# One pass with a running maximum for two 16-head cross attentions

## The reference

```python
# L0: 8 heads of 64, keys turned by their place, keys and values projected from the normed context
sim = einsum('bhid,bhjd->bhij', q, k);  attn = softmax(sim);  out = einsum('bhij,bhjd->bhid', attn, v)
# L1: 16 heads of 16
kp, vp = ctx @ wk.T + bk, ctx @ wv.T + bv
scores = einsum('bhqd,bhkd->bhqk', qh, kh) / 4 - 10000.0 * (1.0 - mask[:, None, None, :])
# L2: 8 heads of 128, no softmax: a cosine of f_q and f_k mixed with products of variances
# L3: 16 heads of 16, no projections: keys and values are the context itself
sim = einsum('bhqd,bhkd->bhqk', q, k) / 4 + (-1e9) * (~mask)[:, None]
```

## Time and profile before

| what | us |
|---|---|
| median of three runs (lowest, highest) | 3203.61 (3202.01, 3211.06) |
| the profiled run, its time | 3209.38 |
| its span, first to last instruction | 3207.2 |
| TensorE busy | 2561.2 (80%) |
| VectorE busy | 1870.5 (58%) |
| ScalarE busy | 1337.1 (42%) |
| GpSimd busy | 563.4 (18%) |
| mean granted TensorE clock | 0.914 of 2.4 GHz |

### The profile page before, as it was taken

The page is one execution under the profiler, slowest core; times in us unless marked ns, Lnnn a source line. Parts: engine busy times, 40 slices in busy tenths (PEclk is TensorE's granted clock), DMA queues, the critical chain, the costliest instruction groups (busy, mean ns, idle before and its releaser), DMA issues. The chain is left out here.

```text
span 3207.2 us, 58901 instructions
## 1 busy us (share of the span) xinstructions
PE 2561.2 (80%) x22154; PEld 1560.7 (49%) x22154; DVE 1870.5 (58%) x2677; ACT 1337.1 (42%) x1802; POOL 563.4 (18%) x331
## 2 busy tenths in 40 slices
PE   3488789999747676799984789999953588699987
PEld 3333346666446232366653645655643333356546
DVE  7599877777662798611114178878847699611111
ACT  2277642222232566467761222222201365466652
POOL 0044420000001343200000023343312244100000
PEclk7799999999879999899995999999976799899999
DMA  7455634443125335467742410100010345568746
GB/s 232 140 182 182 217 104 103 103 94 88 51 69 184 120 119 149 115 138 160 160 97 73 168 47 23 34 23 23 12 39 28 117 141 154 136 148 174 164 103 212
DMA packets 251728, 370.92 MB, mean 116 GB/s; under 512 B 30116, under 2 KB 222055, under 8 KB 251517
## 3 DMA queue, kind: packets, MB, share of 16 engines
q1 hardware_dynamic: 251648, 369.83, 41.5%
HBM read 292.07 MB, written 77.71 MB: 115 GB/s over the span
## 5 line engine op out<-in xcount | busy, mean ns | idle before, releaser
L1870 PE MATMUL l2x_kf<-l2x_w,l2x_nin 128*128 128x512 f32 x784 | 340.5, 594 | 4.2 <-DVE l2x_f L1821 3.4
L1915 POOL TENSOR_TENSOR l2x_gk<-l2x_f,l2x_ks 128x1024 f32<-128x1024 f32 x98 | 182.3, 1896 | 830.2 <-DVEq L1846 830.2
L1180 ACT ACTIVATE l1x_att_pt<-l1x_att_ps,l1x_mask_col 128x1024 f32<-128x1024 f32 x196 | 218.1, 1113 | 99.7 <-PE l1x_att_ps L1235 95.4
L1183 ACT ACTIVATE l3x_att_pt<-l3x_att_ps 128x1024 f32<-128x1024 f32 x196 | 200.4, 1023 | 103.2 <-PE l3x_att_ps L1239 103.0
L1856 ACT ACTIVATE l2x_fsq<-l2x_f 128x1024 f32<-128x1024 f32 x98 | 103.6, 1057 | 330.0 <-DVE l2x_f L1821 330.0
L1870 PEld LDWEIGHTS l2x_kf<-l2x_w,l2x_nin 128*128 128x128 f32 x784 | 147.7, 190 | 188.5 <-issue 180.9
L1172 ACT ACTIVATE l0x_att_pt<-l0x_att_pt 128x1024 f32<-128x1024 f32 x99 | 104.7, 1057 | 300.4 <-DVE l0x_att_pt L1119 300.4
L658 DVE TENSOR_REDUCE l1x_max_red<-l1x_max_ps 128x2 f32<-128x896 f32 x196 | 203.8, 1079 | 37.9 <-PE l1x_max_ps L836 36.7
L815 PE MATMUL l0x_max_pk<-l0x_max_xin,l0x_wk 128*128 128x448 f32 x448 | 197.4, 566 | 29.8 <-DMA l0x_max_xin<-scratch_nT 14.8
L836 PE MATMUL l3x_max_ps<-l3x_max_kp,l3x_qb 128*128 128x448 bf16 x448 | 162.9, 364 | 64.6 <-DVE l3x_max_red L658 26.3
L1140 DVE TENSOR_TENSOR l1x_att_v<-l1x_att_pv,l1x_bv 128x256 f32<-128x256 f32 x98 | 41.6, 424 | 291.6 <-PE l1x_O L1260 281.0
(11 more groups left out here) (689 smaller groups left out, 5259.9 us busy)
## 6 DMA issues: line engine op xcount, KB each, us to landing
l1x_att_kt<-scratch_KS SPq DMA_DIRECT2D x84, 448.0 KB, 8.9
l3x_att_kt<-scratch_KS SPq DMA_DIRECT2D x84, 448.0 KB, 8.6
scratch_KT<-l0x_max_kf SPq DMA_DIRECT2D x28, 896.0 KB, 5.5
l0x_att_kt<-scratch_KT SPq DMA_DIRECT2D x56, 448.0 KB, 7.1
scratch_KS<-l1x_max_kp SPq DMA_DIRECT2D x28, 672.0 KB, 3.7
scratch_KS<-l3x_max_kp SPq DMA_DIRECT2D x28, 672.0 KB, 3.5
l0f_w<-L_ffn_exp_w SPq DMA_DIRECT2D x16, 1024.0 KB, 6.1
l1f_w<-L_ffn_W SPq DMA_DIRECT2D x16, 1024.0 KB, 6.4
```

The costliest lines, as they stand in the source:

```text
L1180: ins = act.activation(pt[u][:, :, :], psc[u][:, :, :].rearrange("p a (b q) -> p (a b) q", q=P), ACT.Exp, bias=tile_ap)
L1183: ins = act.activation(pt[u][:, :, :], psc[u][:, :, :].rearrange("p a (b q) -> p (a b) q", q=P), ACT.Exp)
L1870: last = pe.matmul(pf[u][:, n, :], nin[b][:, c, t * P:(t + 1) * P], w[:, c, n * BANK:(n + 1) * BANK], start=(c == 0), stop=(c == DC - 1))
L1915: pool.tensor_tensor(gk[b][:, t, :, 0:HD], f[b][:, t, :].rearrange("p (h d) -> p h d", h=H), ks[b][:, 2, t, :].unsqueeze(2).broadcast_to([ ...
```

## The change

- `find_maximum` and `attend` are no longer called for L1 and L3. A new class `Heads16` makes one pass of 14 chunks with a running maximum. A chunk has 28 slots of four heads (exponentials of 512 elements). In between stand 16 maximum units a chunk, spread over slots 0, 1, 3, 5, 7, 8, 10, 12 of each half: eight for the later half of the next chunk's heads, eight for the first half of the chunk after it. A unit is one head against 896 keys: two matmuls of 32 rows, in two row groups and two banks, and one fused add (of the mask) and maximum on VectorE, which starts from the maximum so far.
- Once a chunk the new maximum is turned, split and sent through DRAM into the second of two query stacks; the exponential of the difference is spread by four matmuls, copied out by ScalarE, and VectorE multiplies `O` by it before the first weighing of the chunk.
- The bf16 scores for the maxima come from the high part of the keys, loaded from DRAM. So the parts of L1's keys are made ahead, in the loop of the 8-head attention's `attend` (class `SplitKeys`, with its projection), and those of L3 in the loop of the third cross attention. There each has one set of buffers.
- The rows of ones are filled by GpSimd in the setup blocks. The query rows go to two buffers. The mask parts of L1 and `mask3` fall away; the mask's bias goes to DRAM and comes back per chunk, spread over all partitions. In L3 the values are copied by GpSimd, a chunk at a time.

```diff
 class QueryRows:
...
-        parts_to_rows(sp, self.rows, self.scratch, PARTS_OF_Q, self.S.sem("q_in"))
+        for rows in self.rows:
+            parts_to_rows(sp, rows, self.scratch, PARTS_OF_Q, self.S.sem("q_in"))
...
 def attend(...)          # sync: the loads of the next chunks
+                side.load(sp, 0)
                 with sp.Fori(0, steps - 1) as i:
                     for b in range(2):
+                        side.spill(sp, 2 * i + b)
+                        side.load(sp, 2 * i + b + 1)
                         after(sp, sem(f"chunk_used{b}"), i + 1)
...
+                side.finish(sp, 2 * steps)
                          # scalar, behind the exponential of tile t
+                        m, s = 2 * i + t // TILES, t % TILES
+                        if 2 <= s < 6:
+                            side.evacuate(act, m, s - 2)
+                        if s in (3, 5):
+                            side.high(act, m, (s - 3) // 2)
+                        if s == 6:
+                            side.middle(act, m)
                          # tensor
                         weigh(i, t, o)
+                        if 1 <= t % TILES < 5:
+                            side.project(pe, 2 * i + t // TILES, t % TILES - 1)
                          # gpsimd
+                with pool.Fori(0, steps) as i:
+                    for b in range(2):
+                        side.subtract(pool, 2 * i + b)
...
+SLOTS = 4 * TILES
+SPLIT = CHUNK // 2
+HALF_UNITS = 8
+UNIT_SLOTS = tuple(n * SLOTS // 2 // HALF_UNITS for n in range(HALF_UNITS))
+GAP_SLOT, TURN_SLOT, FACTOR_SLOT = SLOTS // 2, 15, 19
+class SplitKeys:
...
+    def load(self, sp, m):
+        if self.proj:
+            after(sp, self.sem("projected"), 4 * m)
+        else:
+            after(sp, self.sem("rest"), m)
...
+        sp.dma_start(self.xin[:, :, :], self.src[bass.ds(m, 1)].squeeze(0)).then_inc(self.sem("xin"), 16)
+    def spill(self, sp, m):
+        after(sp, self.sem("low"), m + 1)
...
+        sp.dma_start(self.dst[bass.ds(m, 1)].squeeze(0), self.kp[:, :, :, :].rearrange(
+            "p s c k -> p (s c) k")).then_inc(self.sem("spilled"), 16)
+    def project(self, pe, m, n):
+        c, side = n // 2, n % 2
+        if n == 0:
+            after(pe, self.sem("xin"), (m + 1) * 16)
+        after(pe, self.sem("read"), 4 * m + n)
+        for d in range(DC):
+            last = pe.matmul(self.px[:, 0:SPLIT], self.w[:, d, c * P:(c + 1) * P],
+                             self.xin[:, d, side * SPLIT:(side + 1) * SPLIT], start=(d == 0), stop=(d == DC - 1))
...
+    def high(self, act, m, c):
+        if c == 0:
+            after(act, self.sem("spilled"), m * 16)
...
+        act.activation(self.kp[:, 0, c, :], self.kf[:, c, :], ACT.Copy).then_inc(self.sem("high"), 1)
+    def middle(self, act, m):
+        after(act, self.sem("rest"), m + 1)
+        act.activation(self.kp[:, 1], self.rest[:, :, :], ACT.Copy).then_inc(self.sem("middle"), 1)
+    def subtract(self, pool, m):
+        after(pool, self.sem("high"), (m + 1) * DC)
+        after(pool, self.sem("low"), m)
+        pool.tensor_tensor(self.rest[:, :, :], self.kf[:, :, :], self.kp[:, 0], ALU.subtract).then_inc(
+            self.sem("rest"), 1)
+        after(pool, self.sem("middle"), m + 1)
+        pool.tensor_tensor(self.kp[:, 2], self.rest[:, :, :], self.kp[:, 1], ALU.subtract).then_inc(
+            self.sem("low"), 1)
...
+class Heads16:
...
+    def ones_rows(self, pool):
+        for b in range(2):
+            pool.memset(self.kt[b][STACK:STACK + 3, :, :], 1.0)
...
+                    def top_to_rows(i, b):          # sync
...
+                        sp.dma_start(rows_dram.rearrange("n h q -> h n q"), parts[:, :, :]).then_inc(
+                            sem("rows_out"), 16)
+                        after(sp, sem("rows_out"), (m + 1) * 16)
+                        sp.dma_start(q_rows[b][STACK:STACK + 3].rearrange("n h q -> n (h q)"),
+                                     rows_dram.rearrange("n h q -> n (h q)")).then_inc(sem(f"rows{b}"), 16)
...
+                    def maximum(i, b, x):           # vector
...
+                        after(dve, sem(f"maxima{x % 2}"), units // 2 * m + x // 2 + 1)
...
+                        dve.tensor_tensor_reduce(junk[x % 2][:, :, :], pm[x % 2][:, :, 0:SPLIT],
+                                                 mrow[b][:, :].rearrange("p (s k) -> p s k", s=2), 1.0,
+                                                 top[1 - b][:, x:x + 1], ALU.add, ALU.max,
+                                                 top[b][:, x:x + 1]).then_inc(sem("max_read"), 1)
...
+                    def body(i, b):
...
+                        after(dve, sem("weighed1"), per * m)
+                        after(dve, sem("F"), m)
+                        dve.tensor_tensor(O[:, :], O[:, :], F[:, :], ALU.mult).then_inc(sem("rescaled"), 1)
...
+                    def body(i, b):                 # scalar
+                        m = 2 * i + b
+                        for s in range(SLOTS):
+                            weights(i, b, s)
+                            if s == TURN_SLOT and exists(i, b, 1):
+                                after(act, sem("gap"), m + 1)
+                                act.activation(fac[:, :, :], gap[:, :].unsqueeze(2).broadcast_to([P, H, 32]),
+                                               ACT.Exp).then_inc(sem("fac"), 1)
+                            if s == FACTOR_SLOT and exists(i, b, 1):
...
+                                act.activation(F[:, :], px[:, :], ACT.Copy).then_inc(sem("F"), 1)
...
+                    def max_unit(i, b, x):          # tensor
...
+                        c, g = x // 8, x % 8 // 2
+                        for side, stationary in enumerate((qb, qb_turned)):
+                            at = (32 * g + 64 * side) % P
+                            last = pe.matmul(pm[x % 2][:, side, 0:SPLIT], stationary[c][at:at + 32, x % 8, :],
+                                             high[b][at:at + 32, c, side * SPLIT:(side + 1) * SPLIT], start=True,
+                                             stop=True)
...
+                    def body(i, b):
...
+                        for s in range(SLOTS):
+                            if s + 1 < SLOTS:
+                                scores(i, b, s + 1)
...
+                            if s in UNIT_SLOTS and exists(i, b, 1):
+                                max_unit(i1, b1, HALF_UNITS + UNIT_SLOTS.index(s))
+                            if s - SLOTS // 2 in UNIT_SLOTS and exists(i, b, 2):
+                                max_unit(*ahead(i, b, 2), UNIT_SLOTS.index(s - SLOTS // 2))
...
+                            weigh(i, b, s)
...
 def l2_xattn(...)        # sync, behind the load of nin for the chunk
+                            side.load(sp, 2 * i + b)
+                            side.spill(sp, 2 * i + b)
```

529 lines of the change are left out of this document (432 added, 97 removed).

## The result

The change makes the kernel a little slower: 3220.7 us (median of 8 runs, 3209.8 to 3226.0) beside 3205.4 us for the kernel before on the same chip, a ratio of 1.0041 with a 95% interval of 1.0027 to 1.0054. The forecast was 3169 us, 35 us faster. The profiled run has a span of 3218.8 us, 11.6 over that of before.

The account below looks back on a forecast made before the run. 16-head maximum passes were taken as VectorE-bound, weighing and 8-head attention as TensorE-bound. Second -118 and set-up +16, fourth -94 and set-up +26, 8-head +130, third +5: -35 us from 3203.6, so 3169 us, own range 3115 to 3225.

Parts of the forecast that it names:

- the wait for `xin`: 8-head attention: next load queues behind the spill, so TensorE stands 2.5 us in 13 chunks, 33 us, bounds 0 and 65.
- what the loop turn gives: 8-head attention: unsized allowance taken off the wait, 38.4 us of chain against a chunk of 35.6, leaving 2.5.
- The projections: 8-head attention: four key projections added to each chunk on TensorE, 6.6 us a chunk, 92 us in all.
- The ends of the stage: 8-head attention: tail of the last spill, 5 us.
- Loop turns and chunk starts: Second attention: TensorE's loss at loop turns and chunk starts, 1.0 us of each 34.5 us chunk.
- Slots, units, the fused reduction, the order of bounds: 16-head loops: slots 0.66 and 0.88 us, maximum unit 0.30, fused add and maximum 1.15; VectorE's work hidden behind TensorE.
- The set-up's 26 us: Fourth attention's set-up: VectorE's chain waits for both GpSimd memsets of the ones rows, 26 us more.
- Third, +5: Third attention: no TensorE work added, but the second chunk's load comes late at the start, +5 us.
- VectorE's sums beside GpSimd's subtractions: 8-head attention: VectorE's sums stand while GpSimd subtracts, with about 3.5 us slack per tile; put at nothing.
- Rival 1: 16-head loops: a maximum unit's two halves run one after the other, 85 less 5 us, 3249 us; chance 0.13.
- Rival 2: 16-head attentions: the fused reduction runs at half speed, 2.0 us, deciding from about 1.8; 3282 us; chance 0.06.
- Rival 3: 8-head attention: the load of `xin` arrives in time, -33 us, 3136 us; chance 0.17.

Follow-up runs that it names:

- only the fourth's half: Kernel before plus one pass in the fourth attention and its key parts in the third's loop, 8-head and second unchanged: 3137.7 us, ratio 0.9780.
- load first: Kernel after, with SyncE issuing the next chunk's key load before it waits for the low part and stores: 3145.2 us, ratio 0.9805.

## Why the prediction was wrong

**The direction** is wrong, by two terms of the sum, both about what stops TensorE between its operations, neither about an operation. They took 62 us, and the fourth attention, 17 us better than forecast, hid a part of it; by that luck the time still lies in the forecast's own range of 3115 to 3225.

- **8-head, the wait for `xin`: mis-sized.** The step "TensorE stands 2.5 us in each of 13 chunks, 33 us, bounds 0 and 65" measured 5.0 us a chunk, 65 us. The chain itself was right: from the fourth projection to the store's issue 13.2 us where the forecast's parts make 13.0, store and load to the next projection 8.7 where they make 8.4. Most of what it left out is the clock: behind the gap the next tile runs 1.6 us slower, and that tile is part of the chain. The two small differences of the chain make 0.5 of the missing 2.5 us, and another 0.3 is what the forecast took off for "what the loop turn gives", which no row shows. The projections, 6.6 us a chunk, measured 6.5. The ends of the stage were 5 in the sum and are about 13.
- **Second, "Loop turns and chunk starts", of which "I keep 1.0 of it a chunk": wrong in kind.** It was taken over from a loop of 1523 instructions that had no fetch at its turns between 1400 and 1635. The new body of 1721 is fetched again at each turn, 3.4 to 4.5 us in which TensorE stands and the slow clock behind it. ScalarE's table load stands at the turns of both kernels, but only in the new one do the turns take longer for it (TensorE waits 1.3 us where no fetch covers it). Mean distance of chunks 36.2 us for 34.5. With TensorE's and ScalarE's loops written out it is 33.0, so the turns cost 3.2 us a chunk where 1.0 stood in the sum. All terms of operations together were 0.5 us too high, and the forecast had the stage right but for this.
- **Slots, units, the fused reduction, the order of bounds:** right, to 0.02 us a slot, 0.01 a unit and to the hundredth for the reduction. VectorE has room in both 16-head loops.
- **Fourth:** chunks of 31.5 and 32.4 us for 33.4; the first, which begins at a clock of 0.50 left from the set-up, takes 38.7. The set-up's 26 us came as forecast, with its cause. What the forecast didn't see is that another cover lay beneath: taking the memsets away brought nothing by itself.
- **Third, +5:** right, 4.7. It is only as good as its place, since the same stage took 8 us more in the kernel with only the fourth's half.
- **VectorE's sums beside GpSimd's subtractions, put at nothing:** their mean went from 1216 to 1817 ns, and VectorE still waited 176.5 us for scores in the same stage. With TensorE at 346 of 350 us in the run with the load first, nothing was right for the time, though the operations did stand.
- **The rivals.** Rival 1 didn't happen; forced, it costs 0.18 us a unit, which comes to 70 us over the chunks where the forecast had 85 less 5, and some 60 more that come with a lower clock. Rival 2: 1.15 us, far from its 1.8. Rival 3 is what load first made: 3145.2 for its 3136. No rival was a cost of code, and none was the clock behind a gap. The wait came out at its upper bound of 65 us, for a reason that the forecast didn't name.

## What to carry to other kernels

In a ring with a single buffer, issue the load when its reader is done, and never behind the wait for a store: the order on SyncE cost 65 us here, and one swapped line gave them back. Size a long loop's body as code, look at the instruction queue in the DMA view at each turn, and write the loop out on the engine that can't afford the jump and on the one that feeds it. When a stall is removed from a set-up, ask what was queued behind it; and count what stands behind each gap of TensorE at the lower clock as part of the gap's price.
